# Attention phase: projections and output halves over four steps, stack reads by pair, maxima reads on SyncE, reciprocals moved

## Chip, cores and metric

One NeuronCore of a Trainium2 chip runs a program of twelve phases. The metric is the device time of one execution in microseconds, the median of the runs of the same kernel. Engines: PE is TensorE, ACT ScalarE, DVE VectorE, POOL GpSimd, SP SyncE, which here issues most DMAs. All run their own instruction streams and meet at semaphores.

## The reference

The whole model is two layers (attention, sparse FFN, a state-space mixer, a mixture of experts). The change touches only the first sub-layer, on 8 batches of 512 tokens, width 256, 16 heads of 16:

```python
q_geo = _rope(_split_heads(x @ Wq_geo.T, H))
k_geo = _rope(_split_heads(x @ Wk_geo.T, H))
v = _split_heads(x @ Wv.T, H)
q = jnp.concatenate([q_sem, q_geo], axis=-1)
k = jnp.concatenate([k_sem, k_geo], axis=-1)
scores = jnp.einsum('bhqd,bhkd->bhqk', q, k).astype(jnp.float32) * scale
scores = jnp.where(causal, scores, jnp.finfo(jnp.float32).min)
attn = jax.nn.softmax(scores, axis=-1).astype(v.dtype)
out = jnp.einsum('bhqk,bhkd->bhqd', attn, v)
return out @ Wo.T
```

x is the layer-normalised input, and the input itself is added at the end (the residual).

## The kernel before

`causal_attention` works through 16 **halves** (batch b, f = 0 or 1: 8 of the 16 heads each), each of 4 **steps** t = 0 to 3. A step handles one **pair** of heads. `batches` writes the order out: two empty halves of lead, eight batches (the middle six in a loop), and a tail. Each engine has its own `step` function; everything else is semaphores, so the order within each `step` is the whole schedule. In each step several stages of different age run side by side:

- **Projections** for the half after the next one (`project`, PE, six 128x512 matmuls each): q plain, q turned, k plain, k turned, and v for the next half. Banks a and c of PSUM hold them. DVE's `turn` multiplies by the rope tables, POOL's `total` adds to y, ACT's `high` and POOL's `rest` split y into a high and a low part (y_hi, y_lo). Columns: +0 and +P are q, +2P and +3P are k, +4P is v.
- **Spread and stack** (SP): `spread_rows` writes three copies of high and low parts, 256 KB each, to the DRAM buffer head_rows; `stack` reads them back as 48 rows a head into qs and ks, two DMAs (e = 0, 1) of 384 KB for all four pairs of a half.
- **Scores** for the pair two steps ahead (`scores`, PE, in three parts j = 0 to 2) wait for q_in and k_in. DVE's `maximum` takes the row maxima, POOL splits them, DVE's `turn_maxima` turns them, ACT writes them to DRAM (`maxima_out`, 16 KB) and reads them back into two rows of qs (`maxima_in`, two DMAs of 4 KB), in the step after.
- **Turned scores** of the step's own pair (`turned_scores`, PE, j = 0 to 2) wait for the maxima (`max_in`); DVE's `keep_past` takes a minimum at the diagonal, ACT's `exponential` writes pt_a, pt_b, pt_c. One PSUM bank pair p_st serves all three, so each part waits for the exponential of the part before.
- **Weighing** (`weigh`, PE) multiplies by v_pad; `take` (ACT) copies out, `gather_sums` (SP) moves the row sums (four DMAs of 32 KB), DVE inverts them in two halves of 256 columns and multiplies (ot_done).
- **Output** of the batch before (`project_out`, PE, eight 128x256 matmuls for each of two parts), with `add_residual` on DVE and, on SP, the store of the result (L291) and the load of the next residual (L294), 512 KB each.

The DMA waits stand on the issuing engine: ACT waits in `maxima_in` until its write has landed, before it goes on to its second exponential.

Of the kernel before, what the change touches and what calls it, by code (L numbers as in the profile page):

```python
# [171 lines left out]
def causal_attention(nc, ctx, src, dst, w_d, wo_d, tables_d, above_d, max_dram, stack_dram, g):  # L172
# [10 lines left out]
    q_in, k_in = ([sem(f"{n}in{f}") for f in range(2)] for n in "qk")  # L183
# [5 lines left out]
    with ExitStack() as mem:  # L189
# [33 lines left out]
        def batches(eng, step):  # L223
# [15 lines left out]
            step(BATCH, 1, 0, BATCH)  # L239
# [5 lines left out]
        def _(sp):  # L245
# [15 lines left out]
            def stack(b, f, kind):  # L261
                tile, arrived = (qs, ks)[kind], (q_in, k_in)[kind][f]
# [11 lines left out]
            def step(b, f, t, n):  # L274
                half = 2 * n + f
                after = (b, 1) if f == 0 else (b + 1, 0)
                if t == 0 and is_half(half + 1):
                    stack(*after, 0)
                    spread_rows(*after, 1)
                if t == 1 and is_half(half + 1):  # L280
                    stack(*after, 1)
                if t == 2 and is_half(half + 2):
                    spread_rows(b + 1, f, 0)
# [4 lines left out]
                if f == 1 and t == 1 and 1 <= n < BATCH:  # L288
# [3 lines left out]
                if f == 1 and t == 2 and 0 <= n < BATCH:  # L292
# [11 lines left out]
        def _(pool):  # L304
# [21 lines left out]
            def step(b, f, t, n):  # L326
# [8 lines left out]
                if t == 1 and is_half(half + 2):  # L335
                    total(b + 1, f, 0)
                if t == 2 and is_half(half + 2):
                    rest(b + 1, f, 0)
                if t == 3 and is_half(half + 2):
# [14 lines left out]
        def _(pe):  # L354
# [31 lines left out]
            def scores(b, f, t, j):  # L386
# [36 lines left out]
            def step(b, f, t, n):  # L423
# [19 lines left out]
                if f == 0 and t == 3 and outs:  # L443
                    if is_half(half + 1):
                        pe.wait_ge(vpad_done, b * 2 + f + 2)
                    pe.wait_ge(ot_done, b * 2)
                    project_out(b, 0, c)
# [11 lines left out]
                if f == 1 and t == 0 and outs:  # L459
                    if is_half(half + 1):  # L460
                        pe.wait_ge(rope_read, counts(1) + 4)
                    pe.wait_ge(res_done, b * 2 - 1)
                    project_out(b, 1, c)
                if t == 1 and is_half(half + 2):
                    at_least(pe, rope_read, counts(1) + 4)
                    if f == 1 and outs:
                        pe.wait_ge(res_done, b * 2)
                    project(b + 1, f * HALF + P, c).then_inc(proj_done, 1)
                if t == 3 and is_half(half + 2):
                    if f == 0 and outs:  # L470
                        pe.wait_ge(res_done, b * 2 - 1)
# [30 lines left out]
        def _(act):  # L502
# [17 lines left out]
            def take(half, quad):  # L520
                act.wait_ge(pv_done, (half * 2 + quad + 1) * FILLS)
                at_least(act, rec_done, half)
# [8 lines left out]

            def maxima_in(b, g_next):
                p = g_next % 2
                f, u = g_next // 4 % 2, g_next % 4
                act.wait_ge(max_out[p], (b * 4 + g_next // 2 + 1) * 16)
                columns = max_dram[p].rearrange("(a c) r -> c a r", a=TPB)
                for e in range(2):
                    at = 64 * e + KS
                    act.dma_start(qs[at:at + 2, f, u, :].bitcast(FP32).rearrange("s (i a r) -> s i a r", i=TPB, a=TPB),
                                 columns[8 * e:8 * e + 8].rearrange("(s i) a r -> s i a r", s=2)).then_inc(max_in[p], 16)  # L540
# [1572 lines left out]
```

## Time and profile before

| | us |
|---|---|
| median of three runs | 6251.31 (6231.87 to 6258.69) |
| profiled execution | 6247.79 |
| its span | 6245.8 |
| PE busy in the span | 5602.4 (90%) |
| DVE, POOL, ACT busy | 4506.1, 3632.0, 3504.9 |
| attention phase, first matmul to last store | 68 to 784 |

Busy time is what an engine works, not what the end waits for. The granted clock of PE is a share of 2.4 GHz; a stretch at 0.50 runs at 1.2 GHz. "Issue" as a releaser means that the engine waited for nothing the profile shows, its own queue's DMA and register commands among it.

### The profile page before, as it was taken

How to read it: one execution, taken by the hardware profiler on the slowest of the kernel's cores; microseconds unless marked ns; L12 is line 12 of the kernel's file. 1: busy time of each engine (PE TensorE's matmuls, PEld its weight loads, DVE VectorE, ACT ScalarE, POOL GpSimd, SP SyncE). 2: the span in 40 equal slices, each digit the busy share in tenths (PEclk: the TensorE clock that was granted, in tenths of full speed). 3: DMA queues.
4: the chain of work that ended last, by engine and by line, in shares of the span. 5: the costliest groups of instructions: out<-in, count | busy, mean ns of one | idle time of the engine just before them, and what ended most of it. 6: DMA issues, size and time to landing. Idle time of an engine off the chain costs nothing. (4 is left out here: it accounts for less than half of the span.)

```text
span 6245.8 us, 127791 instructions
## 1 busy us (share of the span) xinstructions
PE 5602.4 (90%) x40796; PEld 4001.3 (64%) x40796; DVE 4506.1 (72%) x6856; ACT 3504.9 (56%) x4756; POOL 3632.0 (58%) x4101
## 2 busy tenths in 40 slices
PE   5888769647999999999999999999999999985699
PEld 3444347535777777777777777777777777763487
DVE  4666555546888888888888888888888888844444
ACT  2333322225777777777777777777777777731122
POOL 2122100006888888888888888888888888830000
PEclk8778679778999999999999999999999999986799
DMA  3344210121111111111111111111111111121100
GB/s 98 93 103 103 61 58 27 44 95 47 28 31 31 28 31 29 31 29 31 28 34 29 30 28 32 30 28 31 29 31 29 31 28 34 29 87 63 42 24 20
DMA packets 432005, 267.87 MB, mean 43 GB/s; under 512 B 266020, under 2 KB 360804, under 8 KB 430980
## 3 DMA queue, kind: packets, MB, share of 16 engines
q1 hardware_dynamic: 409860, 256.61, 16.1%
q10 hardware_dynamic: 22016, 9.97, 0.6%
q14 instruction: 100, 0.82, 0.0%
q8 instruction: 29, 0.48, 0.0%
HBM read 186.73 MB, written 66.85 MB: 41 GB/s over the span
## 5 line engine op out<-in xcount | busy, mean ns | idle before, releaser
L1568 ACT ACTIVATE ss_r<-ss_pssum,ss_eps 128x512 f32<-128x512 f32 x512 | 353.0, 689 | 901.5 <-PE ss_pssum L1499 901.5
L1628 DVE SCALAR_TENSOR_TENSOR ss_psb<-ss_psb,ss_norm,ss_r 128x512 f32<-128x512 f32 x512 | 362.9, 755 | 446.9 <-ACT ss_r L1570 446.9
L1499 PE MATMUL ss_pssum<-ss_sq,ss_pairssum 128*128 128x512 f32 x1024 | 570.9, 639 | 58.4 <-DVE ss_fr L1616 58.2
L1380 POOL TENSOR_TENSOR ss_sq<-ss_sq 128x512 f32<-128x512 f32 x256 | 330.0, 1289 | 453.9 <-ACT ss_sq L1577 453.9
L48 PE MATMUL ss_psb<-x_hi,ss_whi 128*128 x1024 | 529.3, 517 | 4.4 <-DVE ss_fr L1616 4.4
L1480 PE MATMUL ss_psse<-ss_rot 64*128 64x128 f32 x8224 | 529.5, 279 | 1.2 <-POOL ss_rot L1362 1.2
L1410 POOL TENSOR_TENSOR ss_own<-ident,ss_tk 128x512 f32<-128x512 f32 x512 | 524.4, 1046 | 0.0
L1480 PEld LDWEIGHTS ss_psse<-ss_rot 64*128 64x128 f32 x8224 | 480.2, 188 | 44.4 <-issue 43.0
L48 PE MATMUL ss_psc<-x_hi,ss_whi 128*128 x1024 | 505.4, 494 | 0.0
L1370 POOL TENSOR_TENSOR ss_sq<-ss_sq 128x512 f32<-128x512 f32 x256 | 324.6, 1268 | 137.8 <-ACT ss_sq L1584 137.8
L50 PE MATMUL ss_psb<-x_hi,ss_wlo 128*128 x1024 | 404.0, 394 | 0.0
L49 PE MATMUL ss_psc<-x_lo,ss_whi 128*128 x1024 | 403.6, 394 | 0.0
L50 PE MATMUL ss_psc<-x_hi,ss_wlo 128*128 x1024 | 402.7, 393 | 0.0
L49 PE MATMUL ss_psb<-x_lo,ss_whi 128*128 x1024 | 401.6, 392 | 0.0
L1489 PE MATMUL ss_psm<-ss_xe,ss_bt 128*128 128x16 f32 x3084 | 388.8, 264 | 0.0
L1489 PEld LDWEIGHTS ss_psm<-ss_xe,ss_bt 128*128 128x128 f32 x3084 | 363.8, 191 | 31.2 <-issue 0.2
L1335 POOL MEMSET ss_rot<- 128x4096 f32 x1 | 3.5, 3511 | 651.8 <-POOLq L2049 651.8
L1628 DVE SCALAR_TENSOR_TENSOR ss_psc<-ss_psc,ss_norm,ss_r 128x512 f32<-128x512 f32 x512 | 362.0, 753 | 0.0
L1650 DVE TENSOR_TENSOR ss_gm<-ss_psse,ss_dec 128x1024 f32<-128x1024 f32 x257 | 314.8, 1225 | 41.6 <-POOL ss_dec L1371 41.3
L1570 ACT ACTIVATE ss_r<-ss_r 128x512 f32<-128x512 f32 x512 | 324.2, 633 | 16.7
L1404 POOL TENSOR_TENSOR ss_rot<-ss_rot,ss_tmp 128x512 f32<-128x512 f32 x256 | 332.7, 1300 | 0.0
L1405 POOL TENSOR_TENSOR ss_rot<-ss_rot,ss_tmp 128x512 f32<-128x512 f32 x256 | 332.5, 1299 | 0.0
(347 smaller groups left out, 15658.5 us busy)
## 6 DMA issues: line engine op xcount, KB each, us to landing
ss_dtb<-time_steps SPq DMA_DIRECT2D x516, 128.0 KB, 2.9
ss_wraw<-in_w_state SPq DMA_DIRECT2D x264, 80.0 KB, 2.4
head_rows<-a_yhi SPq DMA_DIRECT2D x64, 256.0 KB, 4.5
a_qs<-head_rows SPq DMA_DIRECT2D x32, 384.0 KB, 5.7
a_ks<-head_rows SPq DMA_DIRECT2D x32, 384.0 KB, 5.5
ss_xp<-x_heads SPq DMA_DIRECT2D x33, 256.0 KB, 4.4
y_heads<-ss_yo SPq DMA_DIRECT2D x132, 64.0 KB, 2.4
head_rows<-a_ylo SPq DMA_DIRECT2D x32, 256.0 KB, 4.5
```

Source lines behind the costliest of these rows:

```text
L48: nc.tensor.matmul(out, w_hi, x_hi, start=first, stop=False)
L49: nc.tensor.matmul(out, w_hi, x_lo, start=False, stop=False)
L50: return nc.tensor.matmul(out, w_lo, x_hi, start=False, stop=last)
L1380: G.tensor_tensor(sq[:, 0, 0], sq[:, 0, 0], sq[:, 0, 1], ALU.add).then_inc(ss_b, 1)
L1404: G.tensor_tensor(rot[:, j, 0], rot[:, j, 0], tmp[:, 0, 0], ALU.add)
L1405: G.tensor_tensor(rot[:, j, 1], rot[:, j, 1], tmp[:, 0, 1], ALU.add).then_inc(rot_b, 1)
L1410: last = G.tensor_tensor(own[:, h * TPB:(h + 1) * TPB], g.ident[:].rearrange("p (o t) -> p o t", o=1).broadcast_to([P, TPB, P]), at_diagon ...
L1480: last = M(p_se[:, h * TPB + c, :], rot[at, 1 - j, e, cols], rot[at, 1 - j, 2 + e, cols], start=e == 0, stop=e == 1)
L1489: last = M(p_m[:, (c * 2 + e) * PW:(c * 2 + e + 1) * PW], bt[:, 2 if e else j, c, :], xe[:, 1 - j, c, :], start=True, stop=True)
L1499: M(p_sum[:], pairs_sum[:], sq[:, q, 0], start=True, stop=True).then_inc((sum_b, sum_c)[q], 1)
L1568: A(r[:, q], p_sum[:], ACT.Ln, scale=1.0 / N1, bias=eps[:, 0:1]).then_inc(ln, 1)
L1628: link.mark(S(bank[:, e, :], bank[:, e, :], norm[:, 2 * q + e:2 * q + e + 1], r[:, q], ALU.mult, ALU.mult))
```

## The change

- SP's `stack` reads q and k of one pair (u) at a time, four DMAs of 96 KB in each step, one step before PE's scores need them. One semaphore per pair (rows_in) takes the place of q_in and k_in.
- `maxima_in` moves from ACT to SP, at the head of SP's step.
- `spread_rows(b + 1, f, 0)`, with ACT's `high` and POOL's `rest` of the q part, goes from t = 2 to t = 3, POOL's `total` from t = 1 to t = 2; the store of the result and the residual load go one step later.
- PE's projection +P goes from t = 1 to t = 2. Output part 0 goes from t = 3 of f = 0 to t = 0 of f = 1, part 1 from t = 0 to t = 1 of f = 1.
- DVE's reciprocals go from the last place of t = 1 and before the third minimum of t = 2 to the places before the second minimum of t = 2 and t = 3; the product that makes ot goes from t = 2 to t = 3. One empty step is added to the tail.

```diff
@@ batches
-            step(BATCH, 1, 0, BATCH)
+            for t in range(2):
+                step(BATCH, 1, t, BATCH)
@@ SP
-            def stack(b, f, kind):
...
-                sp.wait_ge(spread[kind], b * 96 + f * 48 + 48)
-                rows = stack_dram[kind, f].rearrange("(u e r) q -> e r u q", e=2, r=KS)
+            def stack(b, f, u):
+                for kind, tile in ((0, qs), (1, ks)):
+                    if u == 0:
+                        sp.wait_ge(spread[kind], b * 96 + f * 48 + 48)
+                    rows = stack_dram[kind, f].rearrange("(u e r) q -> u e r q", e=2, r=KS)
+                    for e in range(2):
+                        sp.dma_start(tile[64 * e:64 * e + KS, f, u, :].bitcast(FP32), rows[u, e]).then_inc(rows_in[u], 16)
+
+            def maxima_in(b, g_next):
...
+                sp.wait_ge(max_out[p], (b * 4 + g_next // 2 + 1) * 16)
...
                 for e in range(2):
-                    sp.dma_start(tile[64 * e:64 * e + KS, f, :, :].bitcast(FP32), rows[e]).then_inc(arrived, 16)
...
+                    sp.dma_start(qs[at:at + 2, f, u, :].bitcast(FP32).rearrange("s (i a r) -> s i a r", i=TPB, a=TPB),
+                                 columns[8 * e:8 * e + 8].rearrange("(s i) a r -> s i a r", s=2)).then_inc(max_in[p], 16)
@@ SP step
+                if is_pair(4 * half + t + 1):
+                    maxima_in(b, 4 * f + t + 1)
+                if t == 0 and is_half(half):
+                    stack(b, f, 3)
                 if t == 0 and is_half(half + 1):
-                    stack(*after, 0)
                     spread_rows(*after, 1)
-                if t == 1 and is_half(half + 1):
-                    stack(*after, 1)
-                if t == 2 and is_half(half + 2):
+                if t > 0 and is_half(half + 1):
+                    stack(*after, t - 1)
+                if t == 3 and is_half(half + 2):
                     spread_rows(b + 1, f, 0)
@@ PE scores
-                    pe.wait_ge(q_in[f2], b2 * 32 + 32)
-                    pe.wait_ge(k_in[f2], b2 * 32 + 32)
+                    pe.wait_ge(rows_in[u], b2 * 128 + f2 * 64 + 64)
@@ PE step
-                if f == 0 and t == 3 and outs:
...
-                    project_out(b, 0, c)
+                if t == 2 and is_half(half + 2):
...
+                    project(b + 1, f * HALF + P, c).then_inc(proj_done, 1)
...
                 if f == 1 and t == 0 and outs:
...
+                    project_out(b, 0, c)
+                if f == 1 and t == 1 and outs:
                     pe.wait_ge(res_done, b * 2 - 1)
                     project_out(b, 1, c)
-                if t == 1 and is_half(half + 2):
...
-                    project(b + 1, f * HALF + P, c).then_inc(proj_done, 1)
@@ DVE step
+                if t > 1 and is_half(half - 1):
+                    if t == 2:
+                        dve.wait_ge(sums_in, (b * 2 + f) * 128)
+                        at_least(dve, ot_done, b * 2 + f - 1)
+                    part = slice((t - 2) * SEQ // 2, (t - 1) * SEQ // 2)
+                    V.reciprocal(rec[:, part], sums[:, part]).then_inc(rec_done, 1)
                 if here:
                     keep_past(b, f, t, 1)
```

Three places of the instruction order in the loop. **SP**, steps t = 0 and the start of t = 1 of f = 0 (L266 or L268 is the stack, L259 or L260 the spread, L272 or L284 the gather, L277 the maxima). Before:

```order
L266 DMA a_qs<-head_rows 48x4x512 x2
L256 ISA
L259 DMA head_rows<-a_yhi 128x512 x2
L259 DMA head_rows<-a_ylo 128x512
L269 ISA
L272 DMA a_sums<-a_osb 16x512 x4
L266 DMA a_ks<-head_rows 48x4x512 x2
L256 ISA
L259 DMA head_rows<-a_yhi 128x512
L259 DMA head_rows<-a_ylo 128x512
```

Now:

```order
L277 DMA a_qs<-maxima 2x16x32 x2
L268 DMA a_qs<-head_rows 48x512 x2
L268 DMA a_ks<-head_rows 48x512 x2
L257 REGISTER_ALU
L260 DMA head_rows<-a_yhi 128x512 x2
L260 DMA head_rows<-a_ylo 128x512
L281 ISA
L284 DMA a_sums<-a_osb 16x512 x4
L273 ISA
L277 DMA a_qs<-maxima 2x16x32 x2
L265 ISA
L268 DMA a_qs<-head_rows 48x512 x2
```

The q stack of a half is gone from the head of t = 0 and the k stack from t = 1; one pair of both stands behind each read of the maxima.

**ACT**, step t = 0 of f = 0, from the first exponential (pta) to the second (ptb). Before:

```order
L518 ACTIVATE a_pta<-a_psst 128x1024
L529 REGISTER_ALU
L530 DMA maxima<-a_trn 128x32
L543 REGISTER_ALU
L221 ISA
L545 ACTIVATE a_yhi<-a_y 128x512
L535 ISA
L539 DMA a_qs<-maxima 2x16x32 x2
L514 REGISTER_ALU
L221 REGISTER_ALU
L518 ACTIVATE a_ptb<-a_psst 128x1024
```

Now:

```order
L528 ACTIVATE a_pta<-a_psst 128x1024
L539 REGISTER_ALU
L540 DMA maxima<-a_trn 128x32
L543 REGISTER_ALU
L221 ISA
L545 ACTIVATE a_yhi<-a_y 128x512
L524 REGISTER_ALU
L221 REGISTER_ALU
L528 ACTIVATE a_ptb<-a_psst 128x1024
```

The read of the maxima, and the wait ahead of it, no longer stand between the two exponentials.

**DVE**, steps t = 2 and t = 3 of f = 0 (a_psst<-a_psst is the minimum, a_top the maxima, a_t the rope products). Before, the second half of t = 2:

```order
L608 TENSOR_TENSOR a_psst<-a_psst,a_limit 128x2x128 x2
L597 REGISTER_ALU
L601 TENSOR_REDUCE a_top<-a_pss 128x2
L654 RECIPROCAL a_rec<-a_sums 128x256
L608 TENSOR_TENSOR a_psst<-a_psst,a_limit 128x2x128
L597 REGISTER_ALU
L601 TENSOR_REDUCE a_top<-a_pss 128x2
L221 REGISTER_ALU
L667 TENSOR_TENSOR a_ot<-a_oall,a_rec 128x512
L608 TENSOR_TENSOR a_psst<-a_psst,a_limit 128x2x128
```

Now, the middle of t = 3:

```order
L644 RECIPROCAL a_rec<-a_sums 128x256
L606 TENSOR_TENSOR a_psst<-a_psst,a_limit 128x2x128 x2
L221 REGISTER_ALU
L619 REGISTER_ALU
L620 TENSOR_TENSOR a_t<-a_psa,a_tables 128x512
L595 REGISTER_ALU
L599 TENSOR_REDUCE a_top<-a_pss 128x2
L619 REGISTER_ALU
L620 TENSOR_TENSOR a_t<-a_psb,a_tables 128x512
L606 TENSOR_TENSOR a_psst<-a_psst,a_limit 128x2x128
L595 REGISTER_ALU
L599 TENSOR_REDUCE a_top<-a_pss 128x2
```

A reciprocal stood ahead of the third minimum of t = 2; now one stands ahead of the second minimum, in t = 2 and, as here, in t = 3.

## Rows read from the trace of the kernel before

**Rows 1.** View by windows: length, busy us by engine, granted clock, DMA share, GB/s.

```profile
242.00:737.00 495.00, 441.38 (x2398) 233.23 (x2397) 309.17 (x526) 176.94 (x249) 94.52 (x152) 0.77 0.39 93
...
429.00:437.00 8.00, 8.00 (x25) 0.50 0.05 15
```

**Rows 2.** Instructions of line L291, SP's stores: duration, first and last start.

```profile
L291 SPq DMA_DIRECT2D x<-a_outt x7: 411/411/582, 242.2 to 737.2; - x7
```

**Rows 3.** Waits, 112 to 737 us: us in total, times, longest.

```profile
ACT a_ptb L518 <- issue: 31.0, 7, 5.6
PE a_psst L383 <- ACT a_ptb L518: 29.0, 25, 3.7
...
PE a_psst L383 <- DMA a_qs<-maxima: 26.7, 18, 2.8
```

**Rows 4.** Timeline of PE: start, us, instruction [idle before it, what ended it].

```profile
399.25 0.50 PE L383 MATMUL a_psst<-a_qs,a_ks 50*128 50x512 f32 x2
...
409.58 0.50 PE L383 MATMUL a_psst<-a_qs,a_ks 50*128 50x512 f32 x2 [1.72 <-DMA a_qs<-maxima]
...
411.21 0.79 PE L48 MATMUL a_psa<-x_hi,a_whi 128*128 x1
...
426.40 0.66 PE L493 MATMUL a_psb<-ident,a_vt 128*128 128x128 f32 x4
...
478.99 0.49 PE L383 MATMUL a_psst<-a_qs,a_ks 50*128 50x512 f32 x2
...
482.59 0.64 PE L412 MATMUL a_pso<-a_ptc,a_vpad 128*32 128x256 f32 x8
483.16 1.99 PE L420 MATMUL a_psb<-a_wo,a_ot 128*128 128x256 f32 x8
...
485.94 0.50 PE L48 MATMUL a_psa<-x_hi,a_whi 128*128 x1
...
487.52 0.50 PE L383 MATMUL a_psst<-a_qs,a_ks 50*128 50x512 f32 x2
```

**Rows 5.** Timeline of ACT's queue, two steps and an undisturbed one.

```profile
400.43 0.34 ACTq L530 DMA_DIRECT2D maxima<-a_trn  x1
...
410.70 0.36 ACTq L530 DMA_DIRECT2D maxima<-a_trn  x1
415.23 1.26 ACTq L539 DMA_DIRECT2D a_qs<-maxima  x2
...
450.96 0.33 ACTq L530 DMA_DIRECT2D maxima<-a_trn  x1
452.40 1.27 ACTq L539 DMA_DIRECT2D a_qs<-maxima  x2
```

**Rows 6.** Timeline of SP, the same two steps.

```profile
399.62 2.42 SPq L272 DMA_DIRECT2D a_sums<-a_osb  x4
402.17 0.98 SPq L266 DMA_DIRECT2D a_qs<-head_rows  x2
...
410.69 0.81 SPq L266 DMA_DIRECT2D a_ks<-head_rows  x2
```

**Rows 7.** Timeline of SP at the stage's start.

```profile
81.79 0.92 SPq L259 DMA_DIRECT2D head_rows<-a_yhi  x2
...
89.29 0.81 SPq L266 DMA_DIRECT2D a_ks<-head_rows  x2
```

**Rows 8.** Timeline of PE, the first scores.

```profile
96.00 0.37 PE L373 MATMUL a_pss<-a_above,ident 128*128 128x128 bf16 x2 [11.47 <-DMA a_ks<-head_rows]
```

**Rows 9.** Landings by line: L266 at 97, L272 at 399, L259 at 296 us.

```profile
DMA to landing us min/median/max: 4.8/5.6/6.4
...
DMA to landing us min/median/max: 1.9/2.0/2.0
...
DMA to landing us min/median/max: 2.1/2.5/2.7
```

**Rows 10.** Groups by line: the reciprocal (busy us, mean ns, idle before).

```profile
L662 DVE RECIPROCAL a_rec<-a_sums 128x256 f32<-128x256 f32 x16 | 27.9, 1743 | 7.6 <-DMA a_sums<-a_osb 7.6
```

More of the change, by code:

```diff
@@ L182, in causal_attention @@
     spread = [sem(f"{n}spread") for n in "qk"]
-    q_in, k_in = ([sem(f"{n}in{f}") for f in range(2)] for n in "qk")
+    rows_in = [sem(f"rowsin{u}") for u in range(4)]
     turned_done = sem("turned")
@@ L287, in step @@
                     gather_sums(b * 2 + f - 1, 1)
-                if f == 1 and t == 1 and 1 <= n < BATCH:
+                if f == 1 and t == 2 and 1 <= n < BATCH:
                     before = b - 1
@@ L334, in step @@
                     G.tensor_tensor(o_all[:], o_own[:, 0], o_own[:, 1], ALU.add).then_inc(merged, 1)
-                if t == 1 and is_half(half + 2):
+                if t == 2 and is_half(half + 2):
                     total(b + 1, f, 0)
-                if t == 2 and is_half(half + 2):
+                if t == 3 and is_half(half + 2):
                     rest(b + 1, f, 0)
-                if t == 3 and is_half(half + 2):
                     total(b + 1, f, 1)
@@ L442, in step @@
                     project(b + 1, f * HALF, a).then_inc(proj_done, 1)
-                if f == 0 and t == 3 and outs:
-                    if is_half(half + 1):
-                        pe.wait_ge(vpad_done, b * 2 + f + 2)
-                    pe.wait_ge(ot_done, b * 2)
-                    project_out(b, 0, c)
+                if t == 2 and is_half(half + 2):
+                    at_least(pe, rope_read, counts(1) + 4)
+                    if f == 1 and outs:
+                        pe.wait_ge(res_done, b * 2)
+                    project(b + 1, f * HALF + P, c).then_inc(proj_done, 1)
                 if t == 3 and is_half(half + 2):
@@ L521, in take @@
                 act.wait_ge(pv_done, (half * 2 + quad + 1) * FILLS)
-                at_least(act, rec_done, half)
+                at_least(act, rec_done, half * 2)
                 at_least(act, merged, half)
@@ L563, in step @@
                     high(*after, 1)
-                if t == 2 and is_half(half + 2):
+                if t == 3 and is_half(half + 2):
                     high(b + 1, f, 0)
-                if is_pair(4 * half + t + 1):
-                    maxima_in(b, 4 * f + t + 1)
                 if here:
@@ L640, in step @@
                     maximum(b, f, t, 0)
[L641 to L642 removed]
+                if t > 1 and is_half(half - 1):
[4 more added lines that the diff above has]
+                    V.reciprocal(rec[:, part], sums[:, part]).then_inc(rec_done, 1)
                 if here:
                     keep_past(b, f, t, 1)
[L645 removed]
+                if t in (1, 3) and is_half(half + 2):
                     turn(b + 1, f, t // 2, 0)
@@ L648, in step @@
                     maximum(b, f, t, 1)
-                if t % 2 and is_half(half + 2):
-                    turn(b + 1, f, t // 2, 1)
-                if f == 1 and t == 0 and outs:
-                    add_residual(b, 1)
-                if t == 2 and is_half(half - 1):
-                    V.reciprocal(rec[:, SEQ // 2:SEQ], sums[:, SEQ // 2:SEQ]).then_inc(rec_done, 1)
+                if t in (2, 3) and is_half(half + 2):
+                    turn(b + 1, f, t - 2, 1)
+                if f == 1 and t < 2 and outs:
+                    add_residual(b, t)
                 if here:
@@ L658, in step @@
                     maximum(b, f, t, 2)
-                if t == 1 and is_half(half - 1):
-                    dve.wait_ge(sums_in, (b * 2 + f) * 128)
-                    at_least(dve, ot_done, b * 2 + f - 1)
-                    V.reciprocal(rec[:, 0:SEQ // 2], sums[:, 0:SEQ // 2])
-                if t == 2 and is_half(half - 1):
+                if t == 3 and is_half(half - 1):
                     at_least(dve, wo_done, b * 2 if f else b * 2 - 2)
                     dve.wait_ge(merged, b * 2 + f)
-                    dve.wait_ge(rec_done, b * 2 + f)
+                    dve.wait_ge(rec_done, (b * 2 + f) * 2)
                     V.tensor_tensor(ot[:, 1 - f, :], o_all[:], rec[:], ALU.mult).then_inc(ot_done, 1)
```

27 lines of the change are left out of this document (7 added, 20 removed).

## The prediction

> **What bounds the kernel now.** The page comes first: TensorE (PE) is busy nine tenths of the span, so the question is where it is not, and at which clock. The change sits in one stage, the attention phase, 68 to 784 us. The view by windows cuts six of its eight batches out [rows 1]: PE is busy 441.4 of 495 us at a mean granted clock of 0.77. The clock has two levels, 1.00 (2.4 GHz) and 0.50 (1.2 GHz); the second row shows 8 us of pure 0.50 with PE busy throughout. So 0.77 means 46% of the time at 1.2 GHz. SP's stores of the result give the period [rows 2]: 495 us for six batches, 82.5 us a batch, 10.3 us for each of its eight steps.
>
> A batch thus has about 9 us of idle PE and a tax of the slow clock. The waits from 112 to 737 us say what ends the idle time [rows 3]: 26.7 us the read of the maxima into qs, 29.0 us the second exponential (a_ptb). ACT's second exponential is itself held for 31.0 us in "issue", which is ACT's queue standing in the DMA commands ahead of it.
>
> Then single steps [rows 4]. Two steps do the same PE work (t = 0 of f = 1). One runs from 478.99 to 487.52, 8.5 us without a gap, all at 2.4 GHz. The other runs from 399.25 to 409.58, 10.3 us, because the next step's first matmul waited for the maxima. In it SP had put the q stack, twice 384 KB, into the DMA engines at 402.17 [rows 6], just when ACT's read of the maxima was due. In the next step the write of the maxima at 410.70 met the k stack of 410.69, and ACT could issue the read only at 415.23, 4.5 us later; undisturbed it is 1.44 us (450.96 to 452.40) [rows 5, 6]. Small transfers that gate PE stand among bulk transfers, and ACT stands with them.
>
> **The change part by part**, against the profiled execution's 6247.8 us.
>
> *Maxima read by SP.* Two commands of 0.63 us leave ACT's queue for SP's; none is added. SP reads the maxima first in a step, then the stack, then the spread, so bulk of the same step no longer stands ahead. Bulk of the step before still can: a spread after t = 0 and t = 3, and at the end of t = 3 the gather (2.42 us of SP's queue [rows 6]) and, in f = 1, the residual load. The new chain, counted from a step's first matmul S: the write is issued at S+1.2 (399.25 to 400.43 [rows 4, 5]), has landed at S+2.6, SP has issued both reads at S+3.9 (1.27 us), and with the 2.0 us that the 32 KB sums take [rows 9] the data are there at about S+6. No step is that short. So the 26.7 us go, less some 5 us where gather and load are in front: **-22 us** (bounds 0 and -27).
>
> *ACT no longer stands in that read.* Its second exponential starts when the minimum is ready. PE's wait for it is 29.0 us; two thirds of that is plain latency through DVE and ACT and stays, since ACT was held by the queue in only 7 places: **-10 us** (bounds 0 and -29).
>
> *Stack pair by pair.* Per half, 4 commands of 384 KB become 16 of 96 KB: the same bytes, 12 more commands of 0.41 us (0.81 for two [rows 6]). SP issues per half 16 x 0.41 of stack, 4 x 1.27 of maxima, 6 x 0.46 of spread (0.92 for two [rows 7]) and 2 x 2.42 of gather, 19 us in 41 us: it has room. The price is the lead. A pair's rows are read in the step before PE needs them, behind the maxima, and SP issues the last of the four at S+5.1. The trace has no landing of 96 KB. The nearest rows are 2.0 us for 32 KB, and 4.8 and 6.4 us for two reads of 384 KB issued together with nothing behind them [rows 9]. The second 384 KB adds 1.6 us, so bytes are the lesser part; I take 2.8 us, nearer the 32 KB row since 96 KB is nearer to it. Landed at S+7.9 and needed 0.4 us into the next step, that holds a step to at least 7.5 us (6.7 from the short end, 11.1 from the long). Only steps with little PE work are held, and 10.3 us is today's average: **0**, with the long end as a rival.
>
> The Trainium skill's page "DMA: Bandwidth & Descriptors", section "Rules for kernel authors", speaks against this edit: many small transfers should be coalesced into one, as small ones are mostly overhead. By it the sum would be rival 3's; by the rows, where one 0.4 us command follows another while the first is under way, the overheads overlap and the sum stays. The same page, "Issuing engines are not separate DMA queues", has all issuers share the same engines, with only issue time saved by spreading them; the meetings of ACT's and SP's transfers at 402 and 410 us agree.
>
> *Projections and output halves.* PE issues the same matmuls. One projection (1.58 us, 485.94 to 487.52) goes from t = 1 to t = 2; the output halves (1.9 us) go from t = 3 and t = 0 to t = 0 and t = 1 of f = 1. From the step of 8.5 us: without the output half 6.6 (t = 0, f = 0); t = 1 has one weighing of 0.6 us less, 6.0 and 7.9; t = 2 is t = 0 with the transposes (0.66), 7.2; t = 3 is t = 1 with a second projection, 7.6 [rows 4]. In place of steps between 5.7 and 9.5 us: **0** by itself, but it gives PE work while t = 2 waits.
>
> *Reciprocal halves.* Still two of 1.74 us per half [rows 10], now ahead of the second minimum in t = 2 and t = 3, which starts the second exponential. In t = 2 the moved projection covers it. In t = 3 DVE also has both rope products; at worst PE loses the whole 1.74 us in 16 halves (28 us), at best nothing, since one reciprocal stood ahead of a minimum before as well: **+3 us**.
>
> *Start.* The k spread of 81.79 stood behind the q stack's 768 KB and landed only at 89.29; PE's first scores waited for the k stack until 96.00 [rows 7, 8]. Now nothing is ahead of that spread, which then takes 2.1 to 2.7 us [rows 9], and the first pair is a quarter of the bytes: first scores near 90. **-6 us** (0 to -8). At the end one more step without work: 0.
>
> Sum: -22 - 10 + 3 - 6 = **-35 us, so 6212 us**. The profiled execution lies 3.5 us below the median of 6251.3, well inside the spread of the runs. About 0.5%, 31 us, is what a measurement of this kernel can tell from no change: the borders are 6220 and 6283.
>
> **The rivals.**
> 1. *The clock follows.* The sum keeps 46% at 1.2 GHz. The clock falls behind PE's gaps: at 409.58 a gap of 1.72 us ended, and the first matmul of a projection takes 0.79 us at 411.21, against 0.50 at 485.94 [rows 4]. With fewer gaps and a projection in every step the slow share could go to 30%. Half of slow time is tax: 0.16 x 82.5 / 2 = 6.6 us a batch, some 50 us in all, of which the floor of 7.5 us takes a little: 6165 us. Against it: two projections now stand together only in t = 3. Chance 0.20.
> 2. *Waits change their name.* The maxima go, but PE then stands for the exponential behind the reciprocal, or for a write of maxima that meets the spread of the step before. Half of the first two terms is lost and the reciprocals cost 6 us: 6247.8 - 16 + 6 - 6 = 6232 us. This is also the case in which the meetings only move, that is, the change doesn't do what it says. Chance 0.20.
> 3. *Late stacks; this one ends slower.* If 96 KB lands like the median of the large reads, 5.6 us, the rows are there at S+10.7 and no step is under 10.3 us. The steps at 2.4 GHz are now 8.5 and 10.3 us [rows 4], 9.4 in the mean, and about 35 of 64 steps are such: 0.9 x 35 = 31 us. The first two terms are then worth nothing: 6247.8 + 31 + 3 - 6 = 6276 us, and two points more at 1.2 GHz, from the new gaps, add 0.02 x 82.5 / 2 x 8 = 7 us: 6283 us. It decides from a landing of 4.7 us, where the floor is today's 9.4 us. For it: bulk lands in 5 to 6 us here. Against: no bulk of the same step is ahead. Chance 0.15.
>
> **How the numbers follow.** The forecast has 0.45; its own range is 6190 to 6235. Below 6220 lie two thirds of it (0.30), all of rival 1 (0.20) and a little of rival 2 (0.04): faster 0.54. Above 6283 lie half of rival 3 and a little for a clock that falls: slower 0.10. The rest is the same, 0.36. The range 6160 to 6278 leaves out the better half of rival 1 and the worse part of rival 3.
>
> **What would show it.** Right: PE waits for a_qs<-maxima under 8 us; no "issue" ahead of the second exponential; writes of maxima landing in 1.4 to 3 us; first scores near 90 us; a period near 78.5 us. Wrong: PE waiting for a_qs or a_ks<-head_rows at a step's first scores (rival 3); a period under 76 us with a mean clock over 0.83 (rival 1); PE's wait on a_ptb grown past 29 us (rival 2).

## The result and the profile after

The changed kernel takes 6166.8 us (median of 4 runs, 6162.6 to 6179.2) against 6244.7 us (4 runs, 6231.9 to 6258.7): a ratio of 0.9879, 95% interval 0.9854 to 0.9904. That is 78 us or 1.2% less, more than twice the 35 us that were forecast, and within the range. The profiled execution took 6162.61 us, 85.2 us less than that of before.

The period comes first, as in [rows 2]. It is the line of SP's stores of the result:

```profile
L306 SPq DMA_DIRECT2D x<-a_outt x7: 414/420/421, 235.6 to 664.8; - x7
```

Six batches take 429.2 us instead of 495.0: 71.5 us each, 11.0 less. The view by windows over just these six batches, and over two short stretches in them (columns: length, busy time of PE, PEld, DVE, ACT and POOL with instructions, granted clock, DMA share, GB/s):

```profile
235.60:664.80 429.20, 393.31 (x2370) 207.01 (x2370) 309.95 (x521) 177.68 (x250) 95.28 (x152) 0.86 0.35 108
...
403.00:407.00 4.00, 2.45 (x18) 1.12 (x22) 3.21 (x6) 1.62 (x2) 0.00 (x0) 0.97 0.34 101
407.00:413.50 6.50, 6.50 (x37) 2.59 (x30) 3.66 (x6) 1.02 (x1) 0.40 (x2) 0.50 0.03 6
```

Set beside [rows 1], this says where the time went. Before, the 495.0 us were 441.4 us of PE work and 53.6 us of idle PE. Now the 429.2 us are 393.3 of work and 35.9 of idleness. Of the 65.8 us saved, 17.7 are idle time and 48.1 are **busy** time. PE does the same matmuls (the trace shows 2398 and 2370 of them; some records are missing), but faster: the mean granted clock went from 0.77 to 0.86, so from 46% of the time at 1.2 GHz to 28%. Nearly three quarters of the gain in the steady part came through the clock.

PE's waits from 112 to 700 us, which answer to [rows 3]:

```profile
PE a_psst L397 <- ACT a_ptb L528: 35.4, 40, 2.2
PE a_psst L397 <- ACT a_ptc L528: 4.7, 13, 1.3
PE a_pss L387 <- DMA a_ks<-head_rows: 3.0, 4, 1.2
```

The wait for the maxima (26.7 us) is gone, and no "issue" stands ahead of ACT's second exponential any more. The wait for that exponential is 35.4 us against 29.0, but this window reaches into the last batch, where that of [rows 3] does not. In the six batches alone it went from 21.1 us in 18 places to 24.3 in 29, in shorter pieces (the longest was 3.7 us and is 2.2). The list leaves out one wait of 8.9 us behind the seventh store, at the end of the phase, which the kernel before has too (8.7 us). Stacks are hardly ever late. The landings, from issue to arrival (least, median, most), of the write of the maxima and of the 96 KB reads, answer to [rows 9]; each stands under the line of its commands:

```profile
L540 ACTq DMA_DIRECT2D maxima<-a_trn x62: 326/331/349, 113.4 to 662.1; - x62
...
DMA to landing us min/median/max: 1.4/1.5/3.6
```

```profile
L268 SPq DMA_DIRECT2D a_qs<-head_rows x120: 319/418/432, 116.1 to 645.1; - x120
...
DMA to landing us min/median/max: 2.0/2.2/3.3
```

The bytes are the same, but no write of the maxima and no stack takes over 3.6 us; before, a write of the maxima could take 5.0 us, and the 384 KB stacks took 4.4 to 6.9 us. For the small read of the maxima the trace gives no landing. The start, in the timeline of PE, answers to [rows 8]:

```profile
86.76 0.40 PE L387 MATMUL a_pss<-a_above,ident 128*128 128x128 bf16 x2 [5.50 <-DMA a_ks<-head_rows]
```

The first scores begin 9.2 us earlier. Finally a stretch of PE's timeline in the part of the batch that [rows 4] shows: the end of t = 0 of f = 0 (the first two lines), then the thin step t = 1 of f = 0. The number in brackets is the idle time ahead, with its releaser:

```profile
395.63 0.39 PE L397 MATMUL a_psst<-a_qs,a_ks 50*128 50x256 f32 x2 [0.67 <-ACT a_ptb L528]
...
396.49 0.80 PE L48 MATMUL a_psa<-x_hi,a_whi 128*128 x1
...
405.30 0.39 PE L397 MATMUL a_psst<-a_qs,a_ks 50*128 50x256 f32 x2 [1.27 <-ACT a_ptb L528]
405.97 0.29 PE L387 MATMUL a_pss<-a_above,ident 128*128 128x128 bf16 x2 [0.28 <-DVE a_top L599]
...
408.17 0.80 PE L397 MATMUL a_psst<-a_qs,a_ks 50*128 50x512 f32 x2
```

Here the clock still falls. From 403 to 407 us PE works 2.45 of 4 us, and then 6.5 us are at 0.50 without a gap. The matmuls from 408.17 to 412.44 take 4.3 us; at 2.4 GHz the same ones take 2.5 (409.73 to 412.22 in the run with the fuller step, below). At that rate the 6.5 us hold a loss of some 2.7 us, an estimate, behind a gap of 1.3 us. A shorter gap can have slow matmuls behind it too: from 387 to 396.49 PE works 8.74 of 9.49 us at 2.4 GHz, its last gap is 0.67 us, and the projection from 396.49 on is slow, with a clock of 0.54 over 3.7 us. SP at the same place orders its queue as the change says, maxima (L277), then q and k of a pair (L268), with the gather (L284) of the step before ahead of them:

```profile
399.64 2.50 SPq L284 DMA_DIRECT2D a_sums<-a_osb  x4
402.67 1.34 SPq L277 DMA_DIRECT2D a_qs<-maxima  x2
404.14 0.79 SPq L268 DMA_DIRECT2D a_qs<-head_rows  x2
404.97 0.89 SPq L268 DMA_DIRECT2D a_ks<-head_rows  x2
```

### The profile page after: what moved, and what is told of

It is laid out like the page before. It is cut to its first block and busy times, and to the rows that moved or that the text cites. A ratio compares the mean times of both kernels' runs of the same rounds, so it can differ in the third digit from the quotient of the medians.

```text
span 6160.8 us, 127971 instructions
## 1 busy us (share of the span) xinstructions
PE 5549.1 (90%) x40796; PEld 3972.6 (64%) x40796; DVE 4509.5 (73%) x6856; ACT 3505.7 (57%) x4756; POOL 3636.6 (59%) x4101
## 5 line engine op out<-in xcount | busy, mean ns | idle before, releaser
L1400 POOL TENSOR_TENSOR ss_rot<-ss_rot,ss_tmp 128x512 f32<-128x512 f32 x256 | 332.8, 1300 | 0.0
```

Source lines behind the costliest of these rows:

```text
L1400: G.tensor_tensor(rot[:, j, 0], rot[:, j, 0], tmp[:, 0, 0], ALU.add)
```

## The experiments

Theory T, after the result: the size and order of the transfers remove gaps, and the clock follows. Rival E: the evenness of PE's steps (projections and outputs moved) keeps the clock up. Rival Q: ACT's queue, freed of the maxima read, is the gain. Each run stood beside the kernel before on the same chip; its medians were 6239.7 us (first four runs), 6238.0 (next four) and 6245.0 (last three). Intervals in brackets are of the ratio to it. "Six batches" is always the stretch between the first and the last of the seven stores, in the profiled execution. That is one execution, which can lie some us off the median (14 us in one case below); the change itself, profiled twice, has 429.2 and 432.9 us there.

### Transfers alone

The kernel before with the stack by pair and the maxima read at the head of SP's step; no computing is moved.

```diff
@@ SP step
+                if is_pair(4 * half + t + 1):
+                    maxima_in(b, 4 * f + t + 1)
+                if t == 0 and is_half(half):
+                    stack(b, f, 3)
                 if t == 0 and is_half(half + 1):
-                    stack(*after, 0)
                     spread_rows(*after, 1)
-                if t == 1 and is_half(half + 1):
-                    stack(*after, 1)
+                if t > 0 and is_half(half + 1):
+                    stack(*after, t - 1)
@@ ACT step
-                if is_pair(4 * half + t + 1):
-                    maxima_in(b, 4 * f + t + 1)
```

> The kernel before with the DMA parts of the change alone (stack pair by pair, maxima read by SyncE); projections, output halves and reciprocals stay. Theory Order (the waits for the maxima were the gaps that pulled the clock down; without them it stays up): the clock over the six middle batches rises from 0.77 to 0.84 or more, period 73 to 75 us, time 6180 to 6195 us. Theory Spread (the clock rose because PE's work is even over the steps and no step is without a projection): waits for the maxima under 5 us, yet the clock stays at 0.76 to 0.79 and the period at 79 to 81 us, time 6220 to 6235 us.

Measured: 6163.9 us, 0.9876 [0.9859, 0.9892], the whole gain of the change and no less. Its six batches, by the view by windows, and PE's waits from 112 to 700 us:

```profile
233.50:666.30 432.80, 391.78 (x2378) 209.78 (x2378) 303.30 (x522) 176.51 (x249) 94.38 (x152) 0.86 0.35 108
```

```profile
PE a_psst L397 <- ACT a_ptb L531: 21.2, 25, 1.9
PE a_psst L397 <- ACT a_ptc L531: 17.3, 16, 1.3
```

41.0 us idle and the clock at 0.86, in the old order of the computing. That is more than either theory of the expectation allowed, and E falls as the cause: the even steps are not needed for the clock to rise. The moved computing (projection, output halves and reciprocals) adds nothing to the two DMA parts that these runs can tell.

### Computing alone

The changed kernel with both DMA parts undone: stack in halves, maxima read by ACT.

```diff
@@ SP step
-                if is_pair(4 * half + t + 1):
-                    maxima_in(b, 4 * f + t + 1)
...
+                    stack(*after, 0)
                     spread_rows(*after, 1)
+                if t == 1 and is_half(half + 1):
+                    stack(*after, 1)
@@ ACT step
+                if is_pair(4 * half + t + 1):
+                    maxima_in(b, 4 * f + t + 1)
                 if here:
                     exponential(b, f, t, 1)
```

> The changed kernel with its DMA parts undone (stack by half, maxima read by ScalarE); projections, output halves, reciprocals and the q spread stay where the change put them. Theory Order: the waits for the maxima are back at 20 us or more and so is the slow clock, 0.76 to 0.79, time 6230 to 6260 us. Theory Spread: the waits are back, but the clock is 0.83 or more, period 75 to 77 us, time 6190 to 6210 us.

Measured: 6236.6 us, 0.9991 [0.9980, 1.0002]: nothing. Six batches, then waits from 112 to 700 us (PE's two, and ACT's own):

```profile
251.20:732.00 480.80, 415.45 (x2388) 216.48 (x2388) 312.25 (x524) 177.71 (x249) 94.89 (x152) 0.82 0.37 94
```

```profile
PE a_psst L383 <- ACT a_ptb L515: 54.2, 39, 4.5
PE a_psst L383 <- DMA a_qs<-maxima: 20.9, 19, 3.4
...
ACT a_ptb L515 <- issue: 44.0, 9, 5.5
```

Six batches are 14.2 us shorter than before (26 us less PE work, 12 us more idleness: 65.3), yet the medians are only 3 us apart. Most of it is not lost elsewhere: the profiled execution of this run (6237.2 us) lies 10.6 us below that of before (6247.8), and that one lies 8 us above the median that its kernel has beside this run (6239.7). So a good part of the 14.2 us can be the scatter of single executions. Still, the clock rose to 0.82 with more idle time than before, so here it did not follow the idle share.

### Only the maxima read on SP

This is the kernel before; the read moves to the head of SP's step, the stacks stay 384 KB.

```diff
@@ SP step
+                if is_pair(4 * half + t + 1):
+                    maxima_in(b, 4 * f + t + 1)
                 if t == 0 and is_half(half + 1):
                     stack(*after, 0)
@@ ACT step
-                if is_pair(4 * half + t + 1):
-                    maxima_in(b, 4 * f + t + 1)
```

> The kernel before with the read of the maxima moved to SyncE alone, at the head of its step; stack still by half. Theory Order in its weak form (it is enough that the read is issued ahead of the stack and that ScalarE is free): PE's waits for the maxima fall from 26.7 us to under 10 us and the time to 6190 to 6215 us. Rival (the stack by half in one piece delays the write of the maxima in t = 1 as before): waits for the maxima stay at 10 to 20 us, time 6220 to 6245 us.

Measured: 6287.9 us, 1.0074 [1.0058, 1.0091]: **slower** than before, by 48 us. Six batches, PE's waits, SP's timeline of one step, and PE's of its end:

```profile
256.50:779.30 522.80, 447.66 (x2368) 231.79 (x2368) 303.98 (x520) 175.78 (x248) 92.76 (x149) 0.72 0.37 88
```

```profile
PE a_pss L385 <- DMA a_ks<-head_rows: 65.3, 14, 5.6
PE a_psst L395 <- DMA a_qs<-maxima: 5.8, 5, 1.9
```

```profile
428.85 1.34 SPq L275 DMA_DIRECT2D a_qs<-maxima  x2
430.23 0.89 SPq L266 DMA_DIRECT2D a_ks<-head_rows  x2
```

```profile
437.13 0.37 PE L385 MATMUL a_pss<-a_above,ident 128*128 128x128 bf16 x2 [4.58 <-DMA a_ks<-head_rows]
```

The maxima wait all but went (5.8 us are left), and so did ACT's stand, but the k stack now waits on SP behind the maxima and lands 7 us after its issue, 4.6 us too late. Q falls: a free ACT queue by itself is worth less than what the moved wait costs on SP. With 384 KB stacks on SP the read of the maxima should not go there. Neither expectation allowed a slower kernel.

### Only the stack by pair

The kernel before with four 96 KB DMAs a step; the maxima are still read by ACT.

```diff
@@ SP step
+                if t == 0 and is_half(half):
+                    stack(b, f, 3)
                 if t == 0 and is_half(half + 1):
-                    stack(*after, 0)
                     spread_rows(*after, 1)
-                if t == 1 and is_half(half + 1):
-                    stack(*after, 1)
+                if t > 0 and is_half(half + 1):
+                    stack(*after, t - 1)
```

> The kernel before with the stack read pair by pair alone; the maxima are still read by ScalarE. Theory Bulk (the loss was the bulk of 768 KB in one piece in front of the small transfers; who issues the read matters little): PE's waits for the maxima fall from 26.7 us to under 5 us, ScalarE's issue waits from 31.0 us to under 5 us, clock 0.83 or more, time 6160 to 6180 us, all of the gain of the two DMA parts together. Theory Both (the read must also be ahead of the stack and off ScalarE): half of the gain or less, 6195 us or more. Expected with the two lone halves as they are: the other one alone was slower by 48 us, since the stack in one piece then also waited for the maxima.

Measured: 6172.8 us, 0.9896 [0.9879, 0.9912], 65 us of gain. The profiled execution, 6187.3 us, is the slowest of its four, so its numbers are some 14 us on the high side. Six batches, PE's waits, and ACT's own:

```profile
224.00:677.60 453.60, 420.07 (x2384) 227.08 (x2384) 305.78 (x523) 177.51 (x249) 94.48 (x152) 0.80 0.34 103
```

```profile
PE a_psst L385 <- ACT a_ptb L519: 35.2, 29, 2.4
...
ACT a_ptb L519 <- issue: 8.9, 3, 3.0
```

PE's matmuls never wait for the maxima, although ACT still reads them, and ACT's stand fell to 8.9 us. So both waits of before came from the bulk reads in the way, not from the engine that issued the small ones. The edit changes two things at once, the size of a read and how much is put in at one time (768 KB before, 384 KB a step now), and no run tells them apart. This edit alone brings 65 of the 76 us that both DMA parts bring, as the first theory expected, though the clock (0.80) stays short of its 0.83; the interval overlaps that of transfers alone, so what the maxima read on SP adds to it is not settled. The commands per byte rose fourfold and the time fell by 1.0%. The Trainium skill's page "DMA: Bandwidth & Descriptors", "Rules for kernel authors", would have many small transfers coalesced into one, and puts the size below which one pays mostly overhead at 64 KB. The pieces here, 96 KB, lie above it, so the rule says less against this edit than the prediction took it to. In this run a piece lands in 2.4 us (median; 2.0 to 4.3) instead of 4.8 to 6.4 [rows 9], and the DMA engines are busy 0.34 of the time.

### The order on SP

Two orders of the changed kernel: the maxima read last in SP's step, behind stack and spread; and the stack ahead of the maxima read.

```diff
@@ SP step, maxima last
-                if is_pair(4 * half + t + 1):
-                    maxima_in(b, 4 * f + t + 1)
...
                 if t == 3 and is_half(half + 2):
                     spread_rows(b + 1, f, 0)
+                if is_pair(4 * half + t + 1):
+                    maxima_in(b, 4 * f + t + 1)
```

> The changed kernel with one thing moved: SyncE reads the maxima behind the step's stack and spread rather than ahead of them. The same transfers of the same size, the same issuer. Theory Order: the read is again behind bulk (a spread of 768 KB at t = 3 and t = 0, issued some 7 us into the step), PE waits for the maxima there by 1 to 2.5 us in about 30 places, 30 to 60 us, the clock falls below 0.82 and the time is 6200 to 6240 us. Rival Size (96 KB pieces are what counts, the order of the issues little): within 10 us of the changed kernel, 6160 to 6177 us.

Measured: 6203.1 us, 0.9942 [0.9925, 0.9960]. Six batches and PE's waits:

```profile
241.00:702.90 461.90, 416.50 (x2387) 216.34 (x2386) 311.46 (x524) 178.17 (x250) 94.97 (x152) 0.81 0.32 100
```

```profile
PE a_psst L397 <- DMA a_qs<-maxima: 19.9, 12, 3.5
```

The maxima wait is back in 12 places, and some 35 us of the gain are gone. Against the changed kernel's own six batches it is 9.5 us more idleness and 23.2 us more PE work: again the clock (0.81) takes the larger part.

```diff
@@ SP step, stack first
-                if is_pair(4 * half + t + 1):
-                    maxima_in(b, 4 * f + t + 1)
                 if t == 0 and is_half(half):
                     stack(b, f, 3)
-                if t == 0 and is_half(half + 1):
-                    spread_rows(*after, 1)
                 if t > 0 and is_half(half + 1):
                     stack(*after, t - 1)
+                if is_pair(4 * half + t + 1):
+                    maxima_in(b, 4 * f + t + 1)
+                if t == 0 and is_half(half + 1):
+                    spread_rows(*after, 1)
```

> The changed kernel with the step's pair of stack reads issued ahead of the maxima's read (the spread stays behind both). The stack then does not wait for the maxima, so the 8.5 us that PE waited for a_ks<-head_rows go; the read of the maxima has 384 KB in front of it. If landings are set by a fixed part (2.2 us for 96 KB), nothing is lost: 6155 to 6165 us, no wait for maxima over 2 us in total. If the 384 KB delay the write and the read of the maxima as the 768 KB did, PE waits for the maxima 10 us or more and the time is 6175 to 6200 us.

Measured: 6174.9 us, 0.9904 [0.9888, 0.9921]. PE waits 5.5 us in 7 places for the maxima and never for a stack. The intervals of this and of the change overlap, so whether the read of the maxima or the stack goes first is not settled. This run and the one with the maxima last differ only in whether the spread (768 KB, at t = 0 and t = 3) stands ahead of the maxima read, and lie 28 us apart on the same chip: that the read goes before the spread matters.

### The reciprocals in their old places

This is the changed kernel, with the halves back at the end of t = 1 and before the third minimum of t = 2.

```diff
@@ DVE step
-                if t > 1 and is_half(half - 1):
...
-                    part = slice((t - 2) * SEQ // 2, (t - 1) * SEQ // 2)
-                    V.reciprocal(rec[:, part], sums[:, part]).then_inc(rec_done, 1)
...
+                if t == 2 and is_half(half - 1):
+                    V.reciprocal(rec[:, SEQ // 2:SEQ], sums[:, SEQ // 2:SEQ]).then_inc(rec_done, 1)
                 if here:
                     keep_past(b, f, t, 2)
                 if ahead:
                     maximum(b, f, t, 2)
+                if t == 1 and is_half(half - 1):
+                    dve.wait_ge(sums_in, (b * 2 + f) * 128)
...
+                    V.reciprocal(rec[:, 0:SEQ // 2], sums[:, 0:SEQ // 2]).then_inc(rec_done, 1)
```

> The changed kernel with the reciprocals back in their old places (last in t = 1, ahead of the third minimum in t = 2). Tests my term of +3 us for their move. If a reciprocal ahead of the second minimum costs PE its wait on the second exponential: PE's wait on a_ptb falls from 35.4 to about 20 us, the wait on a_ptc grows by 5 to 10 us, time 6155 to 6164 us. If the move was free or paid: 6165 to 6175 us.

Measured: 6214.4 us, 0.9964 [0.9951, 0.9977]. That is 48 us above the change itself (6166.8), so most of its gain is lost, where the expectation had a small gain or none. Six batches, DVE in one t = 2, and PE in the same step:

```profile
248.40:717.70 469.30, 414.57 (x2370) 217.99 (x2370) 308.08 (x521) 175.56 (x249) 95.43 (x152) 0.81 0.32 99
```

```profile
447.13 0.68 DVE L620 TENSOR_TENSOR a_t<-a_psb,a_tables 128x512 f32<-128x512 f32 x1
447.73 1.74 DVE L650 RECIPROCAL a_rec<-a_sums 128x256 f32<-128x256 f32 x1
449.39 0.41 DVE L606 TENSOR_TENSOR a_psst<-a_psst,a_limit 128x256 f32<-128x256 f32 x1
```

```profile
448.04 0.66 PE L503 MATMUL a_psb<-ident,a_vt 128*128 128x128 f32 x4
450.65 0.50 PE L397 MATMUL a_psst<-a_qs,a_ks 50*128 50x512 f32 x2 [1.95 <-ACT a_ptc L528]
```

The moved projection brought its rope product to t = 2, ahead of the third minimum. With the reciprocal there as well, 2.4 us of DVE work stand before it, and PE has only the transposes to do: it stands for 1.95 us, once in a half. All PE's waits for a_ptc from 112 to 700 us come to 25.3 us in 15 places, against 4.7 in the change. So the moved projection makes the moved reciprocals necessary. Moved reciprocals without the moved projection were not run; both together are worth nothing measurable on top of the transfers (6166.8 against 6163.9 with neither).

### A fuller thin step

In the changed kernel, t = 1 of f = 0 has the least PE work. Six matmuls of a projection were added there, into a bank that is free; the values are overwritten later, so this part is computed twice and used once.

```diff
@@ PE step
+                if f == 0 and t == 1 and outs and is_half(half + 2):
+                    pe.wait_ge(rope_read, counts(1) + 4)
+                    project(b + 1, f * HALF + P, c)
                 if f == 1 and t == 0 and outs:
```

> The changed kernel with six projection matmuls more (its result is thrown away, the same projection is made again in the next step) in t = 1 of f = 0 of each batch, where PE has the least work and the clock now falls once in most batches. Theory Clock-by-gaps (the clock falls behind a step in which PE idles over 1.5 us, whoever causes it): the added 1.5 us of work falls into a gap of 1.3 us, the fall at this place goes, the clock rises from 0.85 to 0.90 or more and the time falls by 10 to 30 us to 6135 to 6155 us. Theory Work (the clock depends on the phase and not on this gap, so added work is added time): +1 us a batch, 6170 to 6180 us at a clock of 0.85.

Measured: 6157.1 us, 0.9864 [0.9848, 0.9881]: more work in less time, though the interval overlaps that of the change. Six batches, and the same step as above:

```profile
238.80:660.60 421.80, 397.50 (x2400) 213.19 (x2400) 310.60 (x521) 177.69 (x250) 95.14 (x152) 0.87 0.35 110
```

```profile
406.20 0.50 PE L48 MATMUL a_psb<-x_hi,a_whi 128*128 x1
...
407.78 0.38 PE L397 MATMUL a_psst<-a_qs,a_ks 50*128 50x256 f32 x2
...
409.73 0.50 PE L397 MATMUL a_psst<-a_qs,a_ks 50*128 50x512 f32 x2
```

The gap of 1.27 us is filled (407.78 has none), and the matmul that took 0.80 us behind it takes 0.50: the clock did not fall here. Idle time in six batches is 24.3 us instead of 35.9, busy time 4.2 us more, though six projections of 1.6 us each (406.20 to 407.78) were added. The clock at 0.87 and the gain of 10 us stay short of the 0.90 and the 10 to 30 us expected. The slow stretch ahead of the thin step is still there: at 398.11 PE goes on after 0.67 us of idleness, and from 398.95 to 402.4 its clock is 0.51. So the filler took away one fall, the one behind the gap that it filled, and these rows show no length of gap at which the clock falls. The page "TensorE: Matmul & The Clock Gate" of the Trainium skill, "HAM oscillation", has PE fall to its slow clock again and again when a loop stops it for a transfer, and advises to rearrange the loop so that it stays busy. The traces agree in direction, with gaps as short as this 1.3 us, and here for an exponential rather than a transfer; what they don't show is which such gaps the clock forgives.

### The change again, and other places for the reciprocals

Run together for a close comparison: the change itself; the reciprocals at the end of t = 1 and before the second minimum of t = 3; and that with the fuller thin step.

> The changed kernel itself, beside the two below on the same chip: 6160 to 6175 us. No theory speaks of it; it is the ground for differences of 10 us.

Measured: 6173.2 us, 0.9886 [0.9870, 0.9903] (four runs, 6171.1 to 6174.2), in line with the first measurement.

```diff
@@ DVE step
-                if t > 1 and is_half(half - 1):
...
+                if t == 3 and is_half(half - 1):
+                    V.reciprocal(rec[:, SEQ // 2:SEQ], sums[:, SEQ // 2:SEQ]).then_inc(rec_done, 1)
...
                 if ahead:
                     maximum(b, f, t, 2)
+                if t == 1 and is_half(half - 1):
+                    dve.wait_ge(sums_in, (b * 2 + f) * 128)
...
+                    V.reciprocal(rec[:, 0:SEQ // 2], sums[:, 0:SEQ // 2]).then_inc(rec_done, 1)
```

> The changed kernel with the first reciprocal last in t = 1 and the second ahead of the second minimum of t = 3; t = 2 has none. PE waits 0.78 and 0.22 us in every t = 2 behind the reciprocal there, while the places in t = 1 and t = 3 looked free. Theory Place (a reciprocal costs what its step lacks in cover): about 0.8 us less in each of 16 halves, PE's wait on a_ptb from 35 to under 25 us, 6150 to 6162 us. Rival (the first reciprocal delays the next step's first minimum, and with it the first exponential and the maxima's chain): 6165 to 6185 us.

Measured: 6173.8 us, 0.9888 [0.9871, 0.9904], no difference from the change. PE's wait for a_ptb is 35.2 us in 40 places, against 35.4 in 40: the gain that the first theory expected did not come, and the reciprocal of t = 2 was not what PE waited for.

```diff
@@ both of the edits above
+                if f == 0 and t == 1 and outs and is_half(half + 2):
+                    pe.wait_ge(rope_read, counts(1) + 4)
+                    project(b + 1, f * HALF + P, c)
```

> The same with the six thrown-away projection matmuls of fill6 in t = 1 of f = 0. If both gains are real and add: 15 to 25 us below the changed kernel, 6140 to 6153 us, clock 0.88 or more over the middle batches. If the filler's 10 us were scatter: no better than recip_13.

Measured: 6154.8 us, 0.9858 [0.9842, 0.9875]. Its four runs (6153.9 to 6156.9) lie 14 us and more below all four of the change on the same chip (6171.1 to 6174.2), so the gain of the filler is real: 18 us, or 19 against the same reciprocals without filler (6173.8), within the 15 to 25 us that were expected. Six batches:

```profile
239.20:657.10 417.90, 391.23 (x2400) 209.79 (x2400) 307.65 (x520) 177.10 (x249) 95.03 (x152) 0.88 0.36 111
```

This is the fastest kernel of the study, 1.4% below the kernel before.

| kernel | six batches, us | PE busy | PE idle | clock | median, us |
|---|---|---|---|---|---|
| before | 495.0 | 441.4 | 53.6 | 0.77 | 6244.7 |
| maxima read on SP only | 522.8 | 447.7 | 75.1 | 0.72 | 6287.9 |
| computing alone | 480.8 | 415.5 | 65.3 | 0.82 | 6236.6 |
| reciprocals in old places | 469.3 | 414.6 | 54.7 | 0.81 | 6214.4 |
| maxima read last | 461.9 | 416.5 | 45.4 | 0.81 | 6203.1 |
| stack ahead of maxima read | 437.9 | 400.9 | 37.0 | 0.84 | 6174.9 |
| other reciprocals | 434.1 | 399.3 | 34.8 | 0.84 | 6173.8 |
| the change again | 432.9 | 398.9 | 34.0 | 0.85 | 6173.2 |
| stack by pair only | 453.6 | 420.1 | 33.5 | 0.80 | 6172.8 |
| transfers alone | 432.8 | 391.8 | 41.0 | 0.86 | 6163.9 |
| the change | 429.2 | 393.3 | 35.9 | 0.86 | 6166.8 |
| the change, fuller step | 421.8 | 397.5 | 24.3 | 0.87 | 6157.1 |
| other reciprocals, fuller step | 417.9 | 391.2 | 26.7 | 0.88 | 6154.8 |

## Why the forecast was half of the gain

**The failed step** is the assumption under the whole sum, spelt out under the first rival: "The sum keeps 46% at 1.2 GHz." Waits were priced by their length alone. In six batches the idle time fell by 17.7 us, which for eight is 24 us, against the 29 us of the terms for the maxima, for ACT and for the reciprocals together: that part held in its sum. The clock's share was put at 0 and measured 48.1 us of busy time in six batches, 8.0 us a batch. Rival 1 had it (6.6 us a batch, share 30%, 6165 us) and was given 0.20. It should have been the forecast: [rows 4] already showed a gap of 1.72 us and slow matmuls behind it. What spoke against it, that two projections stand together only in t = 3, did not decide anything: transfers alone reach 0.86 in the old order. The second failed step is the term of 0 for the stack by pair, which alone is worth 65 us (below).

Term by term:

- *Maxima read by SP, -22.* The wait went from 26.7 us to none, so the size held, but not the reason; that the size came right is luck. "Bulk of the same step no longer stands ahead" was credited to the move to SP. The stack by pair alone removes the wait with ACT still reading; the move alone cuts it to 5.8 us and makes the kernel slower. Within the change the order does matter: maxima read last costs some 35 us.
- *ACT no longer stands in the read, -10.* The 31.0 us of "issue" went, but PE's wait for a_ptb, which was to shrink by 10, grew a little (21.1 to 24.3 us in six batches). This is the sign that rival 2 named. With transfers alone it is 15.9 us in six batches and with the stack by pair alone 22.9, so in the old order it is shorter with ACT free of the read, while PE's wait for the third exponential (a_ptc) grew there from 3.1 to 14.7 us. The moves of the computing, not the transfers, made the wait for a_ptb grow; the thin step of t = 1, f = 0 is one such place.
- *Stack by pair, 0.* For a pair a landing of 2.8 us was assumed and 2.2 measured, far from the 4.7 us from which rival 3 decides; rival 3 is out. But the term itself was wrong: this edit alone is worth 65 us. It was costed by its lead only, and its effect on the small transfers was booked under another edit.
- *Projections and output halves, 0.* Computing alone: 0.9991. Held: no gain that the medians show, and none on top of the transfers.
- *Reciprocals, +3.* Wrong in sign, given the moved projection. Without their move the change is 48 us slower, because the moved projection takes its rope product to the same place. The working took the cover of the old place for granted after the cover had changed.
- *Start, -6.* 9.2 measured (96.00 to 86.76 us), beyond the bound of 8.

Of the 85.2 us between the profiled executions the start has 9.2, six batches 65.8, the first and last batches 8.0 (the phase's last store is issued at 693.1 us instead of 776.1), and 2.2 lie outside the phase. One number of the prediction does not follow from its terms: 29 us over eight batches give a period of 78.9 us, not 78.5.

What is open: what sequence of gaps makes the clock fall. The stack by pair alone has the fewest idle microseconds among the kernels without filler (33.5, in a profiled execution that is a slow one) and a clock of only 0.80; computing alone has twice as many and 0.82. So their sum does not decide. Length and place of the gaps are what is left to try, and a gap of 0.67 us in nearly full work, with slow matmuls behind it, speaks against length alone. No run separates the two.

## What to carry to other kernels

Price a gap on PE by its length and by the slow matmuls behind it; where the granted clock of a stage is between its levels, removing waits can be worth a multiple of them (here 65.8 us for 17.7 of idleness), and added matmuls in the thinnest step can pay for themselves. Before a small gating transfer is moved to another queue, cut the bulk transfers that it meets into pieces of the size that the next step needs, and see what then queues behind its wait. When a step of work is moved, look at what its consumers bring to the new place: an order that was harmless there may no longer be.

## What the runs showed of the hardware

- A read of 96 KB lands in 2.2 us (median of 240, 2.0 to 3.3), one of 384 KB in 4.8 to 6.4 us [rows 9]; over all 64 of the kernel before these take 4.4 to 6.9 us. A write of 16 KB takes 1.4 us at the least. The slowest of the kernel before takes 5.0 us, issued with two 384 KB reads and just ahead of a 512 KB store; the slowest of the changed kernel takes 3.6 us, issued 1 to 2 us behind the 768 KB of a spread.
- A gap of 1.27 us was followed by 6.5 us at 1.2 GHz with PE always busy; in the 4 us before these PE worked 2.45. With the gap filled the same stretch stayed at 2.4 GHz. A gap of 0.67 us in nearly full work also had some 3.5 us of slow matmuls behind it, with the filler and without.
- Six more matmuls per batch made the kernel 19 us faster (6154.8 against 6173.8, all else the same).
